# Cross-attention and quantised feed-forward on one core: the weights' transposition moves from TensorE to the DMA queue

## What is computed

```python
scores  = layernorm(x) @ context.T / sqrt(512), masked
atted   = softmax(scores) @ context
x       = x + (atted.T @ W_merge.T + b_merge)

xq      = act_fake_quant(layernorm(x), clip_x)          # one scale over all batches
gate    = xq @ weight_fake_quant(w_gate).T              # w_gate, w_up: 1408 x 512
up      = xq @ weight_fake_quant(w_up).T
h       = act_fake_quant(silu(gate) * up, clip_down)
out     = x + h @ weight_fake_quant(w_down).T           # w_down: 512 x 1408

def weight_fake_quant(w):
    scale = max(abs(w), axis=1, keepdims=True) / 127
    return clip(round(w / scale), -128, 127) * scale
```

## Time and profile before

| | |
|---|---|
| median of 3 runs | 598.17 us |
| the profiled execution's own time | 599.52 us |
| its span, first to last instruction | 597.7 us |
| PE busy | 555.9 us, 93% of the span |
| DVE busy | 456.5 us, 76% |
| ACT busy | 312.4 us, 52% |
| POOL busy | 148.4 us, 25% |
| mean granted TensorE clock | 0.974 of full speed |
| moved by DMA | 78.29 MB, mean 131 GB/s |

### The profile page before, as it was taken

The page is one execution under the profiler, slowest core; times in us unless marked ns, Lnnn a source line. Parts: engine busy times, 40 slices in busy tenths (PEclk is TensorE's granted clock), DMA queues, the critical chain, the costliest instruction groups (busy, mean ns, idle before and its releaser), DMA issues. The chain is left out here.

```text
span 597.7 us, 7947 instructions
## 1 busy us (share of the span) xinstructions
PE 555.9 (93%) x2742; PEld 366.5 (61%) x2742; DVE 456.5 (76%) x839; ACT 312.4 (52%) x461; POOL 148.4 (25%) x77
## 2 busy tenths in 40 slices
PE   5759899999999999999999779999999999699996
PEld 4548688788787787877888534444444444244443
DVE  4278887797788877977766748787878787689884
ACT  3357463555654646457453255566556644786430
POOL 1708434634437345353423100000000000000000
PEclk9969999999999999999999979999999999799999
DMA  8510414233352142412017450643070000669783
GB/s 296 178 72 3 170 70 159 72 120 110 120 194 72 70 159 101 174 48 115 19 67 74 139 191 19 265 154 149 32 263 0 0 0 2 220 263 385 272 284 142
DMA packets 29857, 78.29 MB, mean 131 GB/s; under 512 B 2688, under 2 KB 6784, under 8 KB 27264
## 3 DMA queue, kind: packets, MB, share of 16 engines
q1 hardware_dynamic: 29824, 77.87, 37.5%
HBM read 52.43 MB, written 25.43 MB: 130 GB/s over the span
## 5 line engine op out<-in xcount | busy, mean ns | idle before, releaser
L1226 PE MATMUL gu<-hid,gu_T 128*128 128x512 f16 x704 | 154.6, 381 | 0.8 <-DVE hid L1143 0.8
L1226 PEld LDWEIGHTS gu<-hid,gu_T 128*128 128x128 f16 x704 | 68.7, 98 | 83.4 <-issue 2.1
L1046 ACT ACTIVATE hid<-gu,gu_mul 128x512 f32<-128x512 f32 x88 | 59.6, 685 | 69.6 <-PE gu L1226 64.0
L1124 DVE SCALAR_TENSOR_TENSOR hid<-gu,gu_mul,hid 128x512 f32 (+1 forms) x88 | 65.2, 748 | 40.0 <-PE gu L1226 34.4
L1260 PE MATMUL gu<-wd_T,gu_T 128*128 128x512 f16 x264 | 60.3, 391 | 5.0 <-DVE gu_T L1168 5.0
L774 PE MATMUL mm<-cT_hi,qT_hi 128*128 128x512 f32 x128 | 51.9, 405 | 5.6 <-DVE qT_lo L506 5.6
L568 DVE SCALAR_TENSOR_TENSOR p_lo<-probs,rinv,p_hi 128x512 fp32r<-128x512 f32 x32 | 39.2, 1226 | 21.4 <-ACT p_hi L384 21.0
L342 POOL TENSOR_TENSOR c_lo<-cx,c_hi 128x2048 fp32r<-128x2048 f32 x8 | 37.0, 4623 | 71.4 <-ACT c_hi L412 71.3
L1072 ACT ACTIVATE h<-hid,inv 128x512 int8<-128x512 f32 (+3 forms) x32 | 44.2, 1456 | 19.1 <-DVE gu_T L1168 15.3
L1132 DVE TENSOR_REDUCE hmax<-hid 128x1 f32 (+2 forms) x48 | 53.1, 1120 | 0.0
L774 PE MATMUL mm<-wm_hi,p_hi 128*128 128x512 f32 x128 | 53.1, 415 | 0.0
(11 more groups left out here) (127 smaller groups left out, 953.9 us busy)
## 6 DMA issues: line engine op xcount, KB each, us to landing
h_dram<-hid SPq DMA_DIRECT2D x3, 2816.0 KB, 13.0
hid<-h_dram SPq DMA_DIRECT2D x3, 2816.0 KB, 11.6
cx<-in_ctx_dram SPq DMA_DIRECT2D x7, 1024.0 KB, 7.1
x<-in_x_dram SPq DMA_DIRECT2D x5, 1024.0 KB, 5.5
x_dram<-x SPq DMA_DIRECT2D x20, 256.0 KB, 2.3
xq<-x_dram SPq DMA_DIRECT2D x5, 1024.0 KB, 5.6
x<-x_dram SPq DMA_DIRECT2D x5, 1024.0 KB, 6.5
hid<-x_dram SPq DMA_DIRECT2D x4, 1024.0 KB, 6.5
```

What stands on the lines that cost most here:

```text
L1046: nc.scalar.activation(silu[SILU_AT[i]], gu[2 * (i % 3)][:], ACT.Silu, scale=gu_mul[:, 0, i:i + 1]).then_inc(silu_done, 1)
L1124: nc.vector.scalar_tensor_tensor(hid[:, b % SLOTS, i * L:(i + 1) * L], gu[2 * (i % 3) + 1][:], gu_mul[:, 1, i:i + 1], silu[SILU_AT[i]], AL ...
L1226: last = nc.tensor.matmul(gu[2 * (i % 3) + g][:], gu_T[:, g, h, i * P:(i + 1) * P], xT[p][:, h, :], start=h == 0, stop=h == T - 1)
```

## The change

PE's transposes of the weights and ACT's copies of them out of PSUM are gone, with the semaphore `w_out` and PE's waits on it. In their place SP issues DMA transposes that read `wst16` in SBUF and write `gu_T` and `wd_T` in SBUF (`turn_w`). One transfer turns a 128x512 piece of gate or up (4 blocks), one a 128x1408 piece of down (11 blocks): 22 and 4 transfers in all. In batch n, `turn_w(n - 1)` waits for `w16`, and stands on SP ahead of the mask load and of `load_w(n)`, which now waits for the transfers to land. `turn_w(7)` stands after the first load for the second part, and SP's last wait in attention takes in its landing. `weights_scale`, `weights_round` and `weights16` are as before.

```diff
--- before.py
+++ after.py
@@ helpers of attention()
-                def w_banks(n):
-
-                    gu = [(g, i) for g in range(2) for i in gu_tiles(n)]
-                    half = [("d", 0, DA), ("d", DA, NI)] if n % 2 else []
-                    if not gu:
-                        return [None, None, *half]
-                    return [("gu", g, i) for g, i in gu] + half
...
+                def w_turns(n):
+                    return 16 * rounds(n)
@@ block.sync
+                    def turn_w(n):
+                        sp.wait_ge(w16, n + 1)
+                        for g in range(2):
+                            for i in gu_tiles(n):
+                                sp.dma_start_transpose(gu_T[:, g, :, i * P:(i + 1) * P],
+                                                       wst16[:, gu_columns(n, g, i)]).then_inc(w_done, 16)
+                        if n % 2:
+                            r = down_tile(n)
+                            sp.dma_start_transpose(wd_T[:, :, r * P:(r + 1) * P],
+                                                   wst16[:, down_columns(n)]).then_inc(w_done, 16)
...
                     for n in range(B):
+                        if n:
+                            turn_w(n - 1)
                         if n < B - 1:
                             sp.wait_ge(mneg_made, n + 1)
                             load_mask(n + 1)
                         if n:
-                            sp.wait_ge(w_done, w_count(n - 1, T - 1))
+                            sp.wait_ge(w_done, through(n - 1, w_turns))
                             load_w(n)
...
                     sp.dma_start(xq[:], x1_dram[0].rearrange("p (t d) -> p t d", t=T)).then_inc(x_back, 16)
+                    turn_w(B - 1)
                     sp.wait_ge(scale_stored, 16 * T)
...
                     sp.wait_ge(scale_in, 16)
+                    sp.wait_ge(w_done, through(B - 1, w_turns))
@@ block.scalar
-                    def weights_out(n, k):
...
-                        act.wait_ge(w_done, w_count(n, k))
-                        held = tr[k][:].bitcast(F16)
-                        kind, a, b = bank
-                        if kind == "gu":
-                            nc.scalar.activation(gu_T[:, a, :, b * P:(b + 1) * P],
-                                                 held[:, 0:D].rearrange("p (h r) -> p h r", h=T),
-                                                 ACT.Copy).then_inc(w_out, 1)
...
                             elif t:
                                 probs_hi(n, t - 1)
-                                if t >= 2:
-                                    weights_out(n - 1, t - 2)
                         if not start:
                             probs_hi(n, T - 1)
-                            weights_out(n - 1, 2)
-                            weights_out(n - 1, 3)
...
-                    for k in range(T):
-                        weights_out(B - 1, k)
@@ block.tensor
                                 if n == 1:
                                     pe.wait_ge(wm_ready, g + 1)
-                                elif w_banks(n - 2)[g] is not None:
-                                    pe.wait_ge(w_out, w_count(n - 2, g))
...
-                    def weights(n, k):
...
-                        for h in range(blocks):
-                            last = nc.tensor.transpose(held[:, h * P:(h + 1) * P],
-                                                       wst16[:, at + h * P:at + (h + 1) * P], ident16[:])
-                        last.then_inc(w_done, 1)
...
                             if start:
                                 merge_transpose(k)
-                            else:
-                                for g in ((), (), (0, 1), (2, 3))[k]:
-                                    weights(n - 1, g)
...
-                    for k in range(T):
-                        weights(B - 1, k)
```

More of the change, by code:

```diff
@@ L55, in cross_attention_ffn @@
     SCALE = float(D) ** -0.5
-    DA = (NI + 1) // 2
     assert L == D == 512 and B % 2 == 0 and NI * P == I
@@ L158, in attention @@
                     sem("c_hid"), sem("c_ready"), sem("mneg_made"), sem("resid_ready"))
-                w_maxed, w_step, w_inved, w_rounded, w16, w_done, w_out = (
+                w_maxed, w_step, w_inved, w_rounded, w16, w_done = (
                     sem("w_maxed"), sem("w_step"), sem("w_inved"), sem("w_rounded"), sem("w16"),
-                    sem("w_done"), sem("w_out"))
+                    sem("w_done"))
                 clip_exp, clip_add, clip_rec, clip_made = (
@@ L427, in weights_round @@
                                                  scale=d_inv[:, r:r + 1]).then_inc(w_rounded, 1)
-                    def weights_out(n, k):
-                        bank = w_banks(n)[k]
-                        if bank is None:
-                            return
-                        act.wait_ge(w_done, w_count(n, k))
-                        held = tr[k][:].bitcast(F16)
-                        kind, a, b = bank
-                        if kind == "gu":
-                            nc.scalar.activation(gu_T[:, a, :, b * P:(b + 1) * P],
-                                                 held[:, 0:D].rearrange("p (h r) -> p h r", h=T),
-                                                 ACT.Copy).then_inc(w_out, 1)
-                        else:
[L442 to L445, removed]
                     act.wait_ge(consts, 4)
```

## The result

The changed kernel took 579.25 us, the median of 4 runs (578.79 to 579.51), against 597.95 us before in the same set of runs (596.03 to 598.82). The ratio is 0.968, with a 95% interval of 0.966 to 0.971: faster, by 18.7 us. Forecast were 583.0 us and a range of 580 to 622. The direction and the mechanism were right; the gain of 16.3 us in the sum was too small, and the time came out 3.8 us under the forecast and 0.8 us under the range.

A forecast was written before the change was run, and what follows sets the result against it. PE alone was taken to bound attention, `ffn()` staying at 255 us; 6.5 + 7.1 + 0.7 + 1.3 + 0.7 = 16.3 us off 599.52 gave 583.2, or 581.9 by the median; with 1 us left, 583.0, range 580 to 622.

The forecast's parts named there:

- the sum: Attention: transposes 6.5, idle waits 7.1, restarts 0.7, and 1.3 and 0.7 behind waits, 16.3 us of gain in all.
- What bounds attention: Attention batches: PE alone sets the pace, busy 38.03 of 38.85 us; DVE has 32.35, ACT 21.26.
- The transposes' own cost: PE in attention: 121 transposes on the path at 0.054 us each from start to start, 6.5 us.
- the restarts at eight places: PE behind transpose groups that don't wait: the first matmul costs 0.09 us more at 8 places, 0.7 us.
- The waits: PE's idle time for ACT's copies: 5.4 us into `gu_T` and 1.7 us into `wd_T`, 7.1 us.
- Around them PE loses the restart: Around PE's waits: 0.21 us in six batches, 1.3 us, and 0.15 in five, 0.7 us.
- the sentence on batch 1: Longest PE wait, 2.2 us in batch 1: PE may meet the masked scores there, so 1 us of it was left.
- The price of a transposing transfer: SP's DMA transposes: 2 to 4 us estimated for a transfer, with no such transfer in the trace.
- The first rule of the Trainium skill: DMA transposes: as fast as regular transfers, 350 to 400 GB/s, so the price is low and the change hidden whole.
- if it holds SP in its issue: Sign on SP: the forecast is wrong if a transposing transfer holds SP in its issue; 0.34 to 0.5 us assumed.
- The third rival: Attention's weights loop: transposing transfers become the bound, beyond about 20 us a batch; 604 us up, mostly 610 to 720; chance 0.21.
- The tail: End of attention: `w16` comes some 12 us ahead, one 11-block transfer costs zero; each microsecond over 12 costs 1 or more.

The follow-up runs named there:

- The first kernel: The changed kernel with PE's 132 weight transposes put back, without copies out or waits for them: 587.49 us, ratio to before 0.982.
- the second kernel: The kernel before, with ACT's copies out of the banks moved ahead of the third and fourth exponentials: 587.84 us against 598.27 before, ratio 0.982.
- the third kernel: The kernel before, with ACT's copies moved ahead in batch 1 alone: 594.37 us, ratio 0.993.
- two passes: The changed kernel with every batch's transposing transfers sent twice, the second pass after the first landed: 578.78 us, ratio 0.967.
- the first kernel with three passes: The changed kernel with every batch's transposing transfers sent three times, one pass after the other: 602.43 us, ratio 1.008.
- with the mask ahead: The kernel sending every transposing transfer three times, with the mask load put back ahead of the turning: 596.28 us, ratio 0.997.
- four passes: The changed kernel with every batch's transposing transfers sent four times, one pass after the other: 650.99 us, ratio 1.090.

## Why the prediction was right in kind and short in size

**What bounds attention.** Right. PE alone set the pace before, and sets it after: 36.50 of 36.50 us busy.

**The transposes' own cost.** Right. The sum had 6.5 us, 0.7 for the restarts at eight places, and six further restarts inside what it counted behind the waits: at 0.09 us each some 7.8 us for all fourteen groups. The first kernel shows 7.7 us by the trace, 8.2 by the medians.

**The waits.** This is the step that failed: "Around them PE loses the restart", the term behind the waits, was too small. Without the six restarts of the transposes the sum had 7.1 us of idle time and 1.5 us behind it, 8.6 in all; the second kernel shows 10.4 by the medians and 11.3 by the trace. Two things make up the 2.7 us between 8.6 and 11.3. First, I took the 0.15 to 0.21 us that PE loses around a wait of 0.5 us and applied it to the one of 2.18 us too. Behind that one the granted clock fell, and it cost 1.6 us (the third kernel takes this away with the wait). I had that wait's row in hand; the product behind it should have been read. Second, in batches 2 to 6 I compared only the rows right beside the waits. The kernel with early copies is 1.3 to 1.6 us a batch faster than the kernel before, for 0.8 to 1.1 us of idle time; so 0.5 us a batch go around the waits, where the sum had 0.27. A part of it is a small delay at the context's second transposes, 0.32 us from 114.27 to 114.59 where the kernel with early copies has 0.24, which no row lists as a wait. That is 1.2 us more.

With both the sum is 16.3 + 1.6 + 1.2 = 19.1 us, and the traces gained 19.0 in the batches. On top of this the sentence on batch 1 took a microsecond off the gain, in the one batch where the sum was most too small: it gave 3.3 us and 4.95 came.

**The price of a transposing transfer.** The estimate of 2 to 4 us holds: 2.5 and 3.7. The first rule of the Trainium skill that the prediction weighed, in "Advanced Engine Details and Errata", section X-Bar Transpose (TRN2), can't be tested by these: the landing times of 128 and 352 KB, most of which doesn't grow with the size, show no rate, and by landing time a 128 KB transpose at 2.5 us is near the 256 KB loads' 2.7. The second, the 1309 ns that the Trainium skill gives for one 128x128 block in "VectorE: DVE Perf Modes", section The three transpose paths, is no price per block here: four blocks land in 2.5 us and eleven in 3.7, so (3.7 - 2.5) / 7 = 0.17 us for each further block. What a batch pays is mostly SP's issue, 1.27 us for a 4-block transfer and 1.46 for an 11-block one in the median, one after the other. The sum had 0.34 to 0.5 us for such an issue, and "if it holds SP in its issue" stands among its signs of being wrong. The sign came and the loss didn't: SP is held for some 4 to 6 us a batch and has them to spare.

**Where two errors met.** The mask's load was to go 1.7 us after `wst16` is ready and to land 8.0 us later. In batch 3 it goes after 5.8 us (134.59 to 140.36), for the issues are slow, and POOL has it by 143.44, after 3.1. So 8.9 us stand against 9.7 in the sum, and that POOL waits only 0.45 us is partly luck. DVE was to run 1 us earlier for ACT's lost copies, and runs 0.4 us earlier: `qT_lo` ends 33.8 us after the start of batch 3, where it was 34.25.

**The third rival and its point.** Its mechanism exists, and the change is far from it. The point was put at 20 us of turning a batch. From the first transposing issue to the first issue of the next weights two passes take 12.4 to 14.1 us, and nothing is felt. In the first kernel with three passes they take 19.3 to 21.2 us, and the batches lose 1.2 to 3.1 us each; with the mask ahead they take 19.3 to 22.5 us and lose 0.1 to 2.1. So the point was about right for the transfers, and what the budget left out is POOL's collision with DVE. Beyond the point the slope was wrong: four passes take 25.9 to 27.3 us, 6 to 7 over it, and cost 7.9 to 9.9 us a batch; some 2 us of each batch's loss are the lower clock behind PE's waits. DVE also gets the weights 8.1 us after their first issue (158.2 to 166.3 with three passes, batch 3) where I had 7.0. The mask's load isn't the main reason, for with it ahead the same batch has 7.8; which transfer is stays open. The sentence that POOL "needs no part" of its room was true for one pass.

**The tail.** Right for one transfer. With three, the issues stretch over 15.5 us (323.30 to 338.84), 3.5 more than the 12 of the sum, and PE's wait grows by 7.85; the sum had "1 us or more" for each. The first of the three passes landed only after 10.6 us, where 3.7 is the median; why stays open.

## What to carry to other kernels

When one engine is busy all through a stage, side work that it does for another stage costs its start-to-start time and every wait that it brings; read both, and what the engine does in the twelve instructions behind each long wait. Before moving such work elsewhere, ask whether another engine's program order alone makes the waits: here an earlier place for ACT's copies gave 10.4 of 18.7 us. In this kernel fp16 turns between SBUF tiles were free on a DMA queue with room, up to some 14 us of them a batch; when they took 19 us, it mattered what stood behind them and gated another engine (here the mask). And a mean over seven instructions can be one of 3.05 us and six of 0.17: look at the single ones before a cost is read from it.

## What the runs showed of the hardware

One wait of 2.18 us on a busy PE was followed by 3.3 us at the lower level of the granted clock (kernel before, batch 1), and waits of 0.56 us and less were not. Between the two there is no fixed border by length: one of 1.84 us was followed by it and one of 2.91 us was not (three passes). The waits of 3.9 to 9.8 us of the kernel with four passes all were. A DVE instruction on 128x4 or 128x2 elements, 0.16 or 0.17 us by itself, took 0.9 to 3.3 us when POOL's subtraction on 128x2048 elements ran beside it, and ended 0.02 to 0.03 us after it (three passes). A transposing transfer kept SP in its issue for 1.27 us (4 blocks; 1.20 to 2.09) or 1.46 us (11 blocks; 1.45 to 2.38), some three times as long as a plain one (0.34 to 0.58 us in the rows above). Two passes of transposes next to all other traffic left PE's batches at 36.48 us.
